# Moving the token normalisation and the clamped keys of the second attention from VectorE to ScalarE

## The reference, cut to what matters

```python
def _layernorm(x, axis=-1, eps=1e-05):
    m = jnp.mean(x, axis=axis, keepdims=True)
    v = jnp.var(x, axis=axis, keepdims=True)
    return (x - m) / jnp.sqrt(v + eps)
...
q = jax.nn.softmax(q, axis=-1)      # 12 linear heads of 8 channels
k = jax.nn.elu(k) + 1.0             # = max(k, 0) + exp(min(k, 0))
...
local_out = _local_attn(lq, lk, lv)           # 4 heads, window 128
global_out = _causal_linear_attn(gq, gk, gv)  # 12 heads, blocks of 64
attn = jnp.concatenate([local_out, global_out], axis=1)
return attn @ Wo + bo
```

## Time and profile before

| | |
|---|---|
| median of 3 runs | 1140.09 us (1138.58 to 1140.61) |
| the profiled execution | 1140.24 us, span of its instructions 1138.2 us |
| busy PE, DVE, ACT, POOL | 967.1, 876.1, 737.0, 405.3 us |
| second attention, about | 704 to 925 us of the span |
| step 12 (no gate), step 13 (gate) | 10.97 us, 12.90 us |

### The profile page before, as it was taken

One profiled execution on the slowest core, in us unless ns is written; L12 is line 12 of the kernel. 1 busy time (PEld: TensorE's weight loads), 2 busy tenths in 40 slices (PEclk: granted clock), 3 DMA queues, 4 the chain that ended last, 5 costly groups with the idle time before them and its releaser, 6 DMA issues. The chain is left out here.

```text
span 1138.2 us, 28921 instructions
## 1 busy us (share of the span) xinstructions
PE 967.1 (85%) x10222; PEld 615.8 (54%) x10222; DVE 876.1 (77%) x2339; ACT 737.0 (65%) x1411; POOL 405.3 (36%) x572
## 2 busy tenths in 40 slices
PE   4999999957779999999999895888888618889885
PEld 2788878743444444444444342565655416777742
DVE  5988998837889998788898885788888645667633
ACT  2666666638798888888888782565555306667624
POOL 3545454433531000000100002246677672555533
PEclk9999999968999999999999997899899558999998
DMA  8233322000013000322222211001111012222134
GB/s 265 103 115 121 109 101 71 4 8 12 1 37 104 1 1 12 114 83 74 66 75 74 71 32 31 29 22 38 49 43 44 23 46 75 64 73 62 52 105 138
DMA packets 60219, 72.59 MB, mean 64 GB/s; under 512 B 8858, under 2 KB 36764, under 8 KB 60080
## 3 DMA queue, kind: packets, MB, share of 16 engines
q1 hardware_dynamic: 51312, 60.05, 17.0%
q0 software_dynamic: 4544, 8.60, 2.3%
q10 hardware_dynamic: 4224, 2.10, 0.7%
HBM read 40.14 MB, written 31.49 MB: 63 GB/s over the span
## 5 line engine op out<-in xcount | busy, mean ns | idle before, releaser
L795 ACT ACTIVATE d__hf<-d__HB,dense__d 128x512 f32<-128x512 f32 x288 | 184.9, 679 | 50.1 <-PE d__HB L1021 45.6
L854 DVE TENSOR_TENSOR d__hl<-d__hf,d__hh 128x1024 f16<-128x1024 f32 x144 | 175.2, 1223 | 24.4 <-ACT d__hh L800 22.4
L800 ACT ACTIVATE d__hh<-d__hf 128x1024 f16<-128x1024 f32 x144 | 152.2, 1057 | 4.6
L768 POOL TENSOR_SCALAR d__rstd<-d__mv 128x4 f32<-128x4 f32 x16 | 14.7, 917 | 367.9 <-DVE d__mv L978 367.9
L1019 PE MATMUL d__YB<-d__hh,d__w2h 128*128 128x512 f16 x288 | 109.8, 381 | 23.5 <-DVE d__hl L854 23.5
L1236 POOL DMA_INDIRECT parts<-c__ys,c__dest x78 | 82.1, 1053 | 80.7 <-ACT c__ys L1263 33.8
L1019 PE MATMUL d__HB<-d__xh,d__w1h 128*128 128x512 f16 x288 | 110.3, 383 | 0.0
L1020 PE MATMUL d__HB<-d__xl,d__w1h 128*128 128x512 f16 x288 | 110.1, 382 | 0.0
L1021 PE MATMUL d__HB<-d__xh,d__w1l 128*128 128x512 f16 x288 | 109.9, 382 | 0.0
L1020 PE MATMUL d__YB<-d__hl,d__w2h 128*128 128x512 f16 x288 | 109.7, 381 | 0.0
L1021 PE MATMUL d__YB<-d__hh,d__w2l 128*128 128x512 f16 x288 | 109.7, 381 | 0.0
(11 more groups left out here) (384 smaller groups left out, 2543.5 us busy)
## 6 DMA issues: line engine op xcount, KB each, us to landing
rows<-a__blank SPq DMA_DIRECT2D x72, 268.0 KB, 3.2
d__G<-gates SPq DMA_DIRECT2D x64, 256.0 KB, 3.1
c__xin<-rows SPq DMA_DIRECT2D x39, 134.0 KB
dense__stage<-e_w SPq DMA_DIRECT2D x16, 256.0 KB, 3.1
b__stage<-e_w SPq DMA_DIRECT2D x32, 128.0 KB, 2.3
c__yb<-parts SPq DMA_DIRECT2D x8, 256.0 KB, 8.0
c__yb<-parts ACTq DMA_DIRECT2D x8, 256.0 KB, 8.5
out<-c__xo SPq DMA_DIRECT2D x8, 256.0 KB, 2.3
```

What stands on the lines that cost most here:

```text
L795: act.activation(hf[:, q, f], HB[:, f], gelu, scale=1.0 / WS, bias=b1[:, at:at + 1]).then_inc(s_["h_free"], 1)
L800: act.activation(hh[:, q, f - 1:f + 1], hf[:, q, f - 1:f + 1], ACT.Copy).then_inc(s_["hi_done"], 1)
L854: dve.tensor_tensor(hl[:, q, f], hf[:, q, f], hh[:, q, f], ALU.subtract).then_inc(s_["lo%d_done" % i], 1)
```

## The change

Four edits, all in the second attention:

1. The layer norm's last operation goes from DVE to ACT. DVE now only works out `mean_off = -mean * rstd` (128x2), and ACT does the two tiles as `Identity(rstd * r + mean_off)`.
2. In `PARTS_1` the part `norm` moves up. On DVE it comes before `shift`, on ACT before the exponential of `weights`. PE and POOL have nothing in `norm` or `low`, so their orders stay.
3. The clamped keys go from DVE to ACT: `kn = Relu(-k)` out of the bank, and `ke = exp(-kn)`.
4. DVE takes the query maxima of both banks, waits once, then does both subtractions.

```diff
 PARTS_1 = [
     ...
-    [("weights", 3), ("low", 1), ("shift", 2), ("wide", 1), ("norm", 5), ("gate", 6), ("lower", 0),
+    [("low", 1), ("norm", 5), ("weights", 3), ("shift", 2), ("wide", 1), ("gate", 6), ("lower", 0),
      ("features", 1)],
# ACT, features, for each bank, behind the wait for qd_done
+                        act.activation(kn[:, a], bank[:, GW:2 * GW], ACT.Relu, scale=-1.0).then_inc(s["kn_done"], 1)
                         act.activation(gv[:, a, 0:GW], bank[:, 2 * GW + LH * HD:2 * GW + C], ACT.Copy)
                         act.activation(va[n % 3][:, a, :, 0:HD], ..., ACT.Copy).then_inc(s["keys_done"], 1)
-                        act.activation(ke[:, a], kn[:, a], ACT.Exp).then_inc(s["ke_done"], 1)
+                        act.wait_ge(s["kn_done"], 2 * n + a + 1)
+                        act.activation(ke[:, a], kn[:, a], ACT.Exp, scale=-1.0).then_inc(s["ke_done"], 1)
# ACT
+                if what == "norm":
+                    act.wait_ge(s["off_done"], n + 1)
+                    for a in range(2):
+                        ins = act.activation(xa[:, 2 * n + a, :], r[:, a, :], ACT.Identity, scale=rstd[:, a:a + 1],
+                                             bias=mean_off[:, a:a + 1])
+                    ins.then_inc(s["xn_done"], 1)
# DVE, features
-                    wait(dve, s["ke_done"], 2 * n)
                     wait(dve, s["qe_done"], n)
                     for a, bank in enumerate((BC, BD)):
+                        c.inc(dve.tensor_reduce(qm[:, a], bank[:, 0:GW].rearrange("p (h e) -> p h e", e=HD), AX.X,
+                                                ALU.max))
+                    c.wait()
+                    for a, bank in enumerate((BC, BD)):
                         q = bank[:, 0:GW].rearrange("p (h e) -> p h e", e=HD)
-                        c.inc(dve.tensor_reduce(qm[:, a], q, AX.X, ALU.max))
-                        dve.tensor_scalar(kn[:, a], bank[:, GW:2 * GW], 0.0, None, ALU.min)
-                        c.wait()
                         dve.tensor_tensor(qd[:, a]..., q, qm[:, a, :, None]..., ALU.subtract).then_inc(s["qd_done"], 1)
# DVE, join: r must have been read before it is written again
                         dve.wait_ge(s["xb_done"], n - 3)
+                        wait(dve, s["xn_done"], n - 4)
# DVE, norm
                     dve.wait_ge(s["rstd_done"], n + 1)
-                    for a in range(2):
-                        ins = dve.tensor_scalar(xa[:, 2 * n + a, :], r[:, a, :], mv[:, a, 0:1], rstd[:, a:a + 1],
-                                                ALU.subtract, ALU.mult)
-                    ins.then_inc(s["xn_done"], 1)
+                    dve.scalar_tensor_tensor(out=mean_off[:], in0=mv[:, :, 0], scalar=-1.0, in1=rstd[:],
+                                             op0=ALU.mult, op1=ALU.mult).then_inc(s["off_done"], 1)
```

More of the change, by code:

```diff
@@ L1494, in attention_1 @@
         rstd = m.sb("rstd", [P, 2])
+        mean_off = m.sb("mean_off", [P, 2])
         x3T = m.sb("x3T", [P, TB])
@@ L1533, in attention_1 @@
                  "low_done s_full mx_own max_done mpad_done back_full norm_own ob_done ctx_full ctx_own "
-                 "ctx_done qt_full qt_done mt_full q2_done st_full exp_done wide_full "
+                 "ctx_done kn_done qt_full qt_done mt_full q2_done st_full exp_done wide_full "
                  "qd_done ke_done keys_done kf_done qe_done q_own qr_done pv_full ots_done lin_full lin_done xb_done "
-                 "r_own var_done pool_ln rstd_done xn_done high_rows rows_done lg_own lg_done ld_done le_done rank_own "
+                 "r_own var_done pool_ln rstd_done off_done xn_done high_rows rows_done lg_own lg_done ld_done le_done rank_own "
                  "eq_done rank_done chosen_done gk_done sc_own slot_done words_done scaled "
```

## The result

The changed kernel took 1157.54 us in the median of 4 runs (1150.69 to 1165.78), the kernel before beside it 1139.34 us (1137.06 to 1140.61, 4 runs). The ratio is 1.0145, with a 95% interval from 1.010 to 1.019. The change makes the kernel slower, as forecast (1152.3 us, range 1147 to 1161). The four runs lie in two groups, 1150.7 and 1150.7, 1164.4 and 1165.8. The profiled execution is one of the first pair: 1150.7 us, span 1148.9 us, 10.7 us longer than before.

A forecast was written before the change was run, and what follows sets the result against it. Bound: DVE in gate steps, a DVE-PE ring in steps without `gate`, where `values` would wait for the late exponential. Terms 7.8 + 0.3 + 0.4 + 0.4 + 1.3 + 1.9 = 12.1 us slower, giving 1152.3 us, range 1147 to 1161.

The forecast's parts named there:

- The chain from `mean_off` to `values`: Second attention: hop to ACT 0.16, two tiles 0.70, exponential 1.45, hop to PE 0.25, together 2.56 us.
- All of it is paid: Steps without `gate`: the whole delay of `values` lengthens the step, 7.8 us over steps 5, 6, 8, 12, 14, 16.
- Gate steps: DVE's saving is eaten by the longer ACT chain: 0.1 us lost in each of steps 9, 11, 13, 15.
- `features` starts 0.35 earlier: Gate steps: DVE gives away norm's tiles (0.51 us) for `mean_off` (0.16), so `features` starts at 843.29, not 843.64.
- Steps 1 to 4: Before `norm` begins, two extra ACT instructions of 0.17 us in each step's chain cost 1.3 us.
- Cost nothing by itself: Edit 4 and the new wait in `join`: no cost of their own.
- Steps 17, 18 and the tail: `values` 0.95 us late in step 17, 1.9 us for both; the tail adds nothing and keeps the delay.
- The clock did not go down: Rival: the gap before `values` lowers PE's clock in steps without `gate`, six times 1.0 us, 1158 us; chance 0.2.
- VectorE as the bound: Rival: the exponential does not release `values`, so DVE's savings shorten the steps by 7.4 us, 1132.8 us; chance 0.08.
- second table load: Rival: Relu lies in another table set, so loads repeat for 82 us, 1234 us; chance 0.03.
- It evens out: Rival: cheaper tiles and hops, gate steps win 0.2 us, loss about 6 us or less; chance 0.05 for within 0.2%.
- What would show it: Exponential 0.9 us after `mean_off`, steps without `gate` 12.3 us, gate steps near 12.9, DVE busy time down 16 us.

The follow-up runs named there:

- norm_only: The kernel before with edits 1 and 2 alone; clamped keys and query maxima stay on VectorE as before. Ratio 1.0038, stage 244.29 us.
- the short split: GpSimd's two split operations on 8 columns of each part instead of 128; kernel before 1.0002, new order alone 0.9989, changed kernel 1.010.
- order_only: The kernel before with edit 2 alone: new order, VectorE still does the normalisation tiles. Ratio 0.9941, stage 238.56 us.
- early_paired: The kernel before with normalisation on ScalarE and early (behind `project`), keys clamped on VectorE, maxima of both banks first. Ratio 0.999, stage 241.40 us.
- keys_only: The kernel before with edits 3 and 4 alone; norm stays on VectorE in its old place. 1160.62 us in 4 scattered runs, stage 241.97 us.
- place_back: The changed kernel with edit 2 alone undone, so ScalarE normalises behind the exponential. Ratio 0.9995, stage 242.58 us.
- norm_early: The changed kernel with `norm` moved further up, right behind `project`. Ratio 1.007, stage 243.73 us.
- maxima_only: The kernel before with edit 4 alone, on the second chip. Ratio 1.0028, stage 239.11 us.
- before_split_short: The kernel before with GpSimd's two split operations on 8 instead of 128 columns of each part, second chip. Ratio 1.0002, stage 237.42 us.

## Why the prediction was right, and where its sum was off

The direction, the mechanism and the total came out; the terms did so only in part. That the total came so near (10.7 us between the two profiles, 12.1 in the sum) is in part luck: steps 5 to 16 lost 4.25 us where the sum had 8.9, and the rest of the kernel lost 6.4 where it had 3.2.

*The chain from `mean_off` to `values`.* Forecast 2.56 us, measured 0.19 + 0.78 + 1.43 + 0.06 = 2.46 in step 12. Two tiles from SBUF hold the exponential back by 0.78 (0.39 each), near the chosen 0.70, which came from tiles in PSUM. The hop to TensorE was 0.06, not 0.25: the row taken for it held more than the hop. `values` came 1.19 us later in the even steps (5.65 to 6.84), forecast 1.30. norm_only shows that edits 1 and 2 alone do this.

*"All of it is paid" in steps without `gate`.* This step failed in size. The sum had 7.8 us for steps 5, 6, 8, 12, 14 and 16. Steps 5 and 6 lost 1.26 and 1.23 as forecast, but 8, 12, 14 and 16 only 0.69 to 0.75: 5.4 us in all. VectorE's start at `linear` had been 0.41 to 0.58 us later than TensorE's product allowed, and the delay ate that slack first. The row was there (1.33 us of wait up to 832.01; the product ended at 831.47), and I didn't lay the two side by side. Where the slack is missing, on the second chip, the even step pays 1.20.

*Gate steps.* Forecast 0.1 us lost in each of 9, 11, 13 and 15; measured 0.52 gained in step 13, 12.90 to 12.38, and 1.7 us over steps 7, 11, 13 and 15. The failed step is "`features` starts 0.35 earlier": it starts 1.0 earlier, because `gof` was no longer stretched (0.57) and `mean_off` held the queue for 0.07 us and not 0.16 (0.44 for 0.35). Where `gof` is not stretched in either kernel, on the second chip with the short split, the gain is 0.06 us. ScalarE's chain did grow as forecast, 1.31 to 1.60 us from the first difference to `keys`. But it didn't set the end. TensorE's product did, behind the exponential: `values` at 7.43 us, before 7.55. Step 9 lost 0.79, at a granted clock of 0.75; in the second profile of the changed kernel it had 1.00 and took 12.38 us. Step 10, down for 0.3 us lost, won 0.22: it had 0.75 before and 1.00 after.

*Steps 1 to 4.* Forecast 1.3 us, measured 3.3 in steps 2 to 4. Step 3 lost 0.56, above the 0.34 of two ScalarE instructions. Steps 2 and 4 lost 1.56 and 1.15 with the clock lower too (0.57 for 0.62, 0.86 for 1.00):

```profile
715.99:726.45 10.46, 9.17 (x36) 5.40 (x36) 6.40 (x21) 4.08 (x17) 2.12 (x4) 0.57 0.09 26
726.45:735.77 9.32, 7.33 (x83) 4.84 (x82) 6.75 (x22) 6.56 (x21) 2.14 (x5) 0.97 0.11 31
735.77:746.22 10.45, 9.65 (x92) 6.81 (x92) 7.81 (x28) 6.21 (x19) 2.10 (x4) 0.86 0.08 25
```

Step 2 also took 10.09 us in norm_only and order_only, which leave the keys alone, so its part can't be put down to the edit. Of steps 3 and 4 a part can. At clock 1.00 norm_only took 8.76 and 9.30 us, early_paired 9.06 and 9.51, keys_only 9.14 and 9.59. early_paired leaves the clamping on VectorE, and `norm` has not begun in these steps: so pairing the maxima costs 0.3 and 0.2 us, and the two extra ScalarE instructions, for which the sum had 0.34, cost 0.08. The rest, 0.2 and 0.9 us, came only where the clock was lower: at 0.97 and 0.86 in the changed kernel, place_back and norm_early (9.30 and 10.47), and at 0.98 and 0.86 in maxima_only (9.27 and 10.42) with edit 4 alone. What the clock hangs on there is open.

*Edit 4.* "Cost nothing by itself" was wrong: it costs 0.2 to 0.3 us in each of steps 3 and 4 and, taken alone, 0.3 us in a gate step (maxima_only), since the first difference comes later and ScalarE with it. In the changed kernel's gate steps the late TensorE product covers it.

*Steps 17, 18 and the tail.* From the step 17 start to GpSimd's `rstd` in the tail it lost 1.3 us (forecast 1.9), and from there to the end another 1.3, for which the sum had nothing; no run took that apart.

*The rivals.* The clock did not go down in the even steps: 1.00 in step 12, and 0.96 over steps 5 to 16 against 0.93 before. It did go down in norm_early, by 0.09 to 0.23 in four of the five from step 8 on. VectorE as the bound is refuted by 16 us more idle time at `linear`. Relu brought no second table load; the Trainium skill's rule (ScalarE: Activation LUTs, Table sets: the hidden batching unit) that relu is a filler in every set agrees with this trace, one load of 1283 ns. "It evens out" was nearer for the even steps than its 0.05 suggests: on the first chip they lost 0.7 each, and the gate steps won more than its 0.2.

*What would show it.* The exponential starts 0.97 us after `mean_off` (forecast 0.9). Even steps take 11.7 us instead of 12.3, gate steps 12.4 instead of 12.9: both too high by the same half microsecond, for two different reasons. VectorE's busy time fell by 11.5 us (876.1 to 864.6), not 16: the sum took whole durations, but neighbours overlap, and the two `kn` instructions of a step, 0.25 us long, held the queue for some 0.16 each; besides, `mean_off` takes 244 ns in the mean instead of 130. The idle time before `keys` went only from 3.8 to 4.4 us.

## What to carry to other kernels

Before work goes to an engine that is "only 55% busy", look at what that engine issues next and who waits for it: here 0.8 us of it, tied to a late producer and placed in front of an exponential, delayed the matmuls by 1.2 us, while the 0.5 us saved on the 88% engine went into waiting in half of the steps. Price the steps of each kind by themselves, and lay the releaser's end beside the start it released; if they are half a microsecond apart, as here on the first chip, a delay may be partly free and a speed-up worth nothing. An edit that moves VectorE's work in time can be worth more or less than the work itself, by what GpSimd does at that moment.

## What the runs showed of the hardware that was not expected

- A VectorE instruction on SBUF lasted several times as long when a GpSimd operation ran beside it or came right behind it: `gof` 0.77 to 0.79 us, ending 0.12 us into a `split` of 0.70 us, 0.32 to 0.34 in front of a split of 0.24 us, 0.22 clear of it. `mean_off`, 0.15 us in step 12, took 0.64 in the tail, beside GpSimd's operation of the same span:

```profile
905.38 0.66 POOL L1610 TENSOR_TENSOR b__xr<-keep__xa,b__xr 128x256 f16<-128x256 f32 x1
905.42 0.64 DVE L1822 SCALAR_TENSOR_TENSOR b__mean_off<-b__mv,b__rstd 128x2 f32<-128x2 f32 x1 [0.29 <-POOL b__rstd L1628]
906.09 0.88 ACT L1687 ACTIVATE keep__xa<-b__r,b__mean_off,b__rstd 128x128 f32<-128x128 f32 x2 [5.38 <-DVE b__mean_off L1822]
```

- ScalarE's 128x128 operation with scale and bias per partition takes 488 ns in the mean from SBUF, 456 from PSUM, and two of them 0.88 us.
- On the first chip a wait for TensorE ended 0.4 to 0.8 us after the matmul's given end in even steps, on the second 0.04 to 0.05, in steps with the same order of work. These ends are modelled. The cause is open.
- The same kernel took 1149 us on one chip and 1110 us on another. In the profiles the difference lies behind the second attention: from the first expert matmul to the end 195 us in the profile before and 199 to 202 in most others of the first chip, 167 us in all four of the second. The stages agree, 237.38 us before and 237.42 in before_split_short.
